# A layer of token mixing, attention and experts: the attention's end as a stage of its own, set-up in three phases, new orders on all queues

## The reference

```python
def attn(x):                                  # x: layernorm of the input
    k = x @ Wk.T; r = x @ Wr.T; v = r
    y = wkv_scan(-exp(time_decay), time_first, k, v)   # recurrence over tokens
    return (sigmoid(r) * y) @ Wo.T
def ffn(x):                                   # x: layernorm of (input + attn)
    h = rmsnorm(x, gamma1)
    q = (h @ Wq + bq); kv = (h @ Wdown + bdown) @ Wup + bup     # 16 heads of 32
    att = softmax(q k^T / sqrt(32)) over the 16 heads of one token
    x = x + (att v) @ Wo + bo
    h2 = rmsnorm(x, gamma2); gate = softmax(h2 @ Wg + bg)       # 8 experts
    return x + sum_e gate_e * (h2 @ We[e])
x = x + attn(layernorm(x)); x = x + ffn(layernorm(x))
```

## Time and profile before

| | |
|---|---|
| median of three runs | 2970.51 us |
| time of the profiled execution | 2970.13 us |
| span in that profile | 2968.3 us |
| PE matmuls busy | 2786.5 us, 94% |
| DVE busy | 2170.1 us, 73% |
| ACT busy | 1294.7 us, 44% |
| POOL busy | 610.0 us, 21% |
| mean granted TensorE clock | 0.975 |

### The profile page before, as it was taken

One profiled execution on the slowest core, in us unless ns is written; L12 is line 12 of the kernel. 1 busy time (PEld: TensorE's weight loads), 2 busy tenths in 40 slices (PEclk: granted clock), 3 DMA queues, 4 the chain that ended last, 5 costly groups with the idle time before them and its releaser, 6 DMA issues.

```text
span 2968.3 us, 47758 instructions
## 1 busy us (share of the span) xinstructions
PE 2786.5 (94%) x18896; PEld 1761.5 (59%) x18896; DVE 2170.1 (73%) x4100; ACT 1294.7 (44%) x2399; POOL 610.0 (21%) x681
## 2 busy tenths in 40 slices
PE   3269999999999999999999999999999999999989
PEld 2146566666666656666665566666556666656644
DVE  4887777877777777777777777777777777787753
ACT  1364454444444444444443444444344445344431
POOL 0122222122222212222221222122122122221210
PEclk9569999999999999999999999999999999999999
DMA  7012221112222112222211122221121221021110
GB/s 216 15 22 30 29 36 28 32 29 30 37 29 36 28 31 30 29 37 29 36 30 29 30 29 37 29 36 30 29 30 29 37 30 36 24 33 25 30 22 15
DMA packets 579074, 102.44 MB, mean 35 GB/s; under 512 B 547346, under 2 KB 547474, under 8 KB 578834
## 3 DMA queue, kind: packets, MB, share of 16 engines
q1 hardware_dynamic: 578852, 99.39, 19.4%
HBM read 48.49 MB, written 16.78 MB: 22 GB/s over the span
## 4 chain that ended last, share of the span: by engine, by line
PE 83%; DVE 6%; SPq 5%; DMA 2%; ACT 2%; issue 1%; POOL 0%; ACTq 0%; DVEq 0%
PE bank L1075 69%; PE bank L1231 8%; PE bank L1105 3%; SPq L439 3%; DVE mcol L987 3%; PE bank L1221 2%; DMA ks<-k 2%; SPq L435 2%; PE bank L1191 1%; ACT t L637 1%; PE bank L1208 1%; DVE mx L725 1%; DVE zz L915 0%; DVE w_e L823 0%; SPq L392 0%
## 5 line engine op out<-in xcount | busy, mean ns | idle before, releaser
L1075 PE MATMUL bank<-w_e,h2t 128*128 128x512 f16 x6144 | 1390.8, 382 | 5.3 <-DVE acc L1055 5.3
L1075 PEld LDWEIGHTS bank<-w_e,h2t 128*128 128x128 f16 x6144 | 598.8, 99 | 686.5 <-issue 17.5
L1055 DVE SCALAR_TENSOR_TENSOR acc<-bank,gates,acc 128x512 f32<-128x512 f32 x512 | 368.0, 729 | 246.3 <-PE bank L1075 245.7
L657 ACT ACTIVATE pr<-bank,col 128x512 f32<-128x512 f32 x256 | 171.6, 683 | 560.7 <-PE bank L1221 560.7
L1231 PE MATMUL bank<-vp,pr 128*128 128x33 f32 x2048 | 267.9, 276 | 5.1 <-ACT pr L657 5.0
L1231 PEld LDWEIGHTS bank<-vp,pr 128*128 128x128 f32 x2048 | 260.1, 196 | 17.3 <-DVE rden L1000 3.6
L476 POOL TENSOR_TENSOR zz<-wkv,zz 128x512 f32<-128x512 f32 x64 | 105.2, 1644 | 772.0 <-DVE ev L902 772.0
L1075 PE MATMUL bank<-w_o,xo 128*128 128x512 f16 x768 | 174.7, 385 | 55.6 <-DVE xo L853 55.6
L915 DVE RECIPROCAL zz<-zz 128x256 f32<-128x256 f32 x128 | 223.1, 1743 | 0.0
L987 DVE TENSOR_REDUCE mcol<-bank 128x4 f32<-128x512 f32 x256 | 155.9, 680 | 39.0 <-PE bank L1208 39.0
L1075 PE MATMUL bank<-w_o,qo 128*128 128x512 f16 x768 | 173.9, 384 | 6.4 <-DVE qo L853 6.4
(11 more groups left out here) (178 smaller groups left out, 3713.3 us busy)
## 6 DMA issues: line engine op xcount, KB each, us to landing
qs<-qo SPq DMA_DIRECT2D x384, 64.0 KB, 3.4
xk<-in_attn_x SPq DMA_DIRECT2D x32, 512.0 KB, 3.7
x<-in_attn_x SPq DMA_DIRECT2D x32, 512.0 KB, 3.7
result<-acc SPq DMA_DIRECT2D x32, 512.0 KB, 2.8
ks<-k SPq DMA_DIRECT2D x128, 64.0 KB, 3.3
w_e<-in_ffn_We SPq DMA_DIRECT2D x7, 1024.0 KB, 14.1
qs<-in_attn_Wk SPq DMA_DIRECT2D x1, 1024.0 KB, 5.8
ks<-in_attn_Wr SPq DMA_DIRECT2D x1, 1024.0 KB, 7.9
```

What stands on the lines that cost most here:

```text
L657: nc.scalar.activation(pr[:, k % 2, :], att_bank[ATT_BANK["S", k]][:, :], ACT.Exp, scale=colof["soft"])\
L1055: V.scalar_tensor_tensor(out=acc[:, s, :], in0=moe_bank[u % 2][:, :], scalar=gates[:, s, e:e + 1], in1=acc[:, s, :], op0=ALU.mult, op1=ALU ...
L1075: ins = nc.tensor.matmul(dst, left(a), right(b), start=(n == 0), stop=(n == last))
```

## The change

1. **A stage of its own.** `att_back`, `att_project`, `att_square`, `att_norm2`, `att_turn2` and `att_gate` become the stage `fin` with counters of its own. Its products O, T2 and G leave the ring of att and use the two mix banks, between V and O of the tile two later. It gets buffers of its own: `on`, `ot` (transposed output, then the second normalised tile) and `oo16`.
2. **Set-up in three phases**: k and r; then o1, q, d, u, o2, g with the constants of the attention; then the experts. Each has its own maxima, reduction over partitions, scales and counters. x and its residual copy are loaded ahead of the weights.
3. **New lists.** Each engine has a head, a repeated body and a tail. An entry (name, k, n) names a tile in the head, and a distance back from i in the body (i from 4 to 30) and from 32 in the tail.
4. The value products stay in float32, as they were.

```diff
+PHASES = [["k", "r"], ["o1", "q", "d", "u", "o2", "g"], [f"e{e}" for e in range(E)]]
+MAXED = ["k", "r", "o1", "q", "o2", "small"] + PHASES[2]
...
-            + [x for k in range(7) for x in (("S", k + 1), ("PV", k))] + [("PV", 7)]
-            + [("O", 0), ("O", 1), ("T2", 0), ("T2", 1), ("G", 0)])
+            + [x for k in range(7) for x in (("S", k + 1), ("PV", k))] + [("PV", 7)])
...
+HEAD_END, TAIL_FROM = 4, -1
...
+    ("mix_project", 0, 3), ("moe", 10, 1), ("moe", 11, 1), ("moe", 12, 1), ("att_turn", 0, 3), ("mix_turn", 0, 4),
+    ("att_latent", 0, 3),
+]
+
 PE_ORDER = [
...
+    ("att_q", 0, 1), ("mix_k", 0, 0), ("att_up", 0, 1), ("mix_v", 0, 0), ("moe", 13, 3), ("fin_project", 0, 2),
+    ("moe", 14, 3), ("att_max", 0, 1), ("att_max", 1, 1), ("moe", 15, 3), ("fin_turn2", 0, 2), ("att_max", 2, 1),
+    ("att_max", 3, 1), ("fin_gate", 0, 2), ("moe", 0, 2), ("att_m", 0, 1), ("moe", 1, 2), ("moe", 2, 2),
+    ("moe", 3, 2), ("att_scores", 0, 1), ("att_scores", 1, 1), ("moe", 4, 2), ("att_probs", 0, 1),
+    ("att_scores", 2, 1), ("att_probs", 1, 1), ("moe", 5, 2), ("att_scores", 3, 1), ("att_probs", 2, 1),
+    ("att_scores", 4, 1), ("moe", 6, 2), ("moe", 7, 2), ("att_probs", 3, 1), ("att_scores", 5, 1),
+    ("att_probs", 4, 1), ("att_scores", 6, 1), ("att_probs", 5, 1), ("att_scores", 7, 1), ("moe", 8, 2),
+    ("att_probs", 6, 1), ("att_probs", 7, 1), ("moe", 9, 2), ("mix_project", 0, 0), ("moe", 10, 2), ("moe", 11, 2),
+    ("moe", 12, 2), ("att_turn", 0, 0), ("mix_turn", 0, -1), ("att_latent", 0, 0),
 ]
...
+DVE_HEAD = [
+    ("set_init", 0, -1), ("pre_stats", 0, 0), ("pre_norm", 0, 0), ("set_max", 0, -1), ("set_max", 1, -1),
+    ("set_scale", 0, -1), ("set_max", 2, -1), ("set_k", 0, -1), ("set_max", 3, -1), ("set_max", 4, -1),
+    ("set_max", 5, -1), ("set_k", 1, -1), ("set_scale", 1, -1), ("set_r", 0, -1), ("set_r", 1, -1),
+    ("mix_turn", 0, 0), ("set_o1", 0, -1), ("set_max", 6, -1), ("set_max", 7, -1), ("set_max", 8, -1),
+    ("set_o1", 1, -1), ("mix_decay", 0, 0), ("set_q", 0, -1), ("set_max", 9, -1), ("set_max", 10, -1),
...
 DVE_ORDER = [
...
+    ("att_max", 3, 3), ("moe_gate", 0, 4), ("moe", 0, 4), ("att_m", 0, 3), ("moe", 1, 4), ("mix_rec", 0, 2),
+    ("moe", 2, 4), ("mix_rec", 1, 2), ("mix_gate", 0, 2), ("moe", 3, 4), ("mix_split", 0, 2), ("mix_decay", 1, 2),
+    ("att_probs", 0, 3), ("att_probs", 1, 3), ("moe", 4, 4), ("moe", 5, 4), ("mix_sum", 1, 2), ("mix_value", 1, 2),
+    ("mix_scan", 1, 2), ("att_probs", 2, 3), ("moe", 6, 4), ("att_probs", 3, 3), ("mix_rec", 2, 2), ("moe", 7, 4),
+    ("att_probs", 4, 3), ("mix_rec", 3, 2), ("mix_gate", 1, 2), ("att_probs", 5, 3), ("mix_split", 1, 2),
+    ("moe", 8, 4), ("att_probs", 6, 3), ("att_probs", 7, 3), ("pre_stats", 0, 1), ("moe", 9, 4),
+    ("mix_project", 0, 2), ("att_stats", 0, 2), ("moe", 10, 4), ("pre_norm", 0, 1), ("att_norm", 0, 2),
+    ("att_turn", 0, 2), ("att_latent", 0, 2), ("mix_turn", 0, 1), ("moe", 11, 4), ("fin_back", 0, 3),
+    ("mix_decay", 0, 1), ("att_stack", 0, 2), ("moe", 12, 4), ("att_vt", 0, 2), ("moe", 13, 4), ("mix_sum", 0, 1),
+    ("mix_value", 0, 1), ("fin_project", 0, 3), ("mix_scan", 0, 1), ("moe", 14, 4), ("att_max", 0, 2),
+    ("att_max", 1, 2), ("moe", 15, 4), ("fin_turn2", 0, 3), ("att_max", 2, 2),
 ]
...
 ACT_ORDER = [
...
+    ("mix_num", 1, 1), ("att_scores", 6, 2), ("att_scores", 7, 2), ("mix_split", 1, 1), ("pre_norm", 0, 0),
+    ("att_norm", 0, 1), ("att_turn", 0, 1), ("mix_turn", 0, 0), ("att_latent", 0, 1), ("att_q", 0, 1),
+    ("fin_back", 0, 2), ("mix_k", 0, 0), ("att_up", 0, 1), ("mix_v", 0, 0),
 ]
...
 POOL_ORDER = [
...
+    ("att_up", 0, 2), ("fin_square", 0, 3), ("mix_sum", 0, 1), ("moe_acc", 0, 3), ("mix_num", 0, 1),
+    ("mix_sum", 1, 1), ("mix_num", 1, 1), ("pre_stats", 0, 0), ("att_rest", 0, 2), ("att_stats", 0, 1),
+    ("att_q", 0, 1),
 ]
...
 SP_ORDER = [
-    ("mix_k", 0), ("att_up", 0), ("att_m", 0), ("pre_load", 0), ("moe_store", 0),
+    ("att_up", 0, 2), ("moe_store", 0, 4), ("att_m", 0, 2), ("mix_k", 0, 1), ("pre_load", 0, 0),
 ]
...
-        on = hrow[:, :].rearrange("p (g d) -> p g d", d=HD)
+        on = sb("on", [P, G, HD])
+        ot = sb("ot", [P, SUB * C])
...
+        oo16 = sb("oo16", [P, 2, CB, T], F16)
...
+        def pipeline(eng, head, order, tail, steps):
...
+            for name, k, n in head:
+                run(name, k, n)
+            for i in range(HEAD_END, NT + TAIL_FROM):
+                for name, k, lag in order:
+                    run(name, k, i - lag)
+            for name, k, lag in tail:
+                run(name, k, NT - lag)
...
+                if name == "small":
+                    dve.wait_ge(smalls_in, 16 * 7)
...
+                    dve.wait_ge(const_in, 16 * CONSTS)
...
-    nc = bacc.Bacc("TRN2", target_bir_lowering=False, num_devices=1)
+    nc = bacc.Bacc("TRN2", target_bir_lowering=False, num_devices=1, dynamic_dma_scratch_size=2048)
```

More of the change, by code:

```diff
@@ L128, in att_before @@
             return ATT_USES[m], True
-PE_ORDER = [
[L134 to L141, removed]
+HEAD_END, TAIL_FROM = 4, -1
@@ L142 @@
 ]
 DVE_ORDER = [
[L145 to L149, removed]
@@ L154 @@
 ]
 ACT_ORDER = [
-    ("mix_turn", 0), ("att_norm", 0), ("moe_gate", 0), ("moe", 0), ("att_turn", 0), ("moe", 1), ("mix_k", 0),
-    ("moe", 2), ("moe", 3), ("att_latent", 0), ("att_q", 0), ("att_up", 0), ("mix_v", 0), ("mix_exp", 0), ("moe", 4),
-    ("moe", 5), ("moe", 6), ("moe", 7), ("att_rest", 0), ("att_scores", 0), ("att_scores", 1), ("moe", 8),
-    ("mix_num", 0), ("mix_split", 0), ("moe", 9), ("att_scores", 2), ("att_scores", 3), ("att_scores", 4),
-    ("mix_exp", 1), ("att_scores", 5), ("moe", 10), ("att_scores", 6), ("att_scores", 7), ("moe", 11),
@@ L162 @@
[L162 to L163 removed]
+    ("mix_exp", 0, 1), ("fin_square", 0, 3), ("fin_norm2", 0, 3), ("fin_turn2", 0, 3), ("mix_num", 0, 1),
+    ("moe_gate", 0, 3), ("att_rest", 0, 2), ("att_scores", 0, 2), ("mix_split", 0, 1), ("att_scores", 1, 2),
+    ("att_scores", 2, 2), ("mix_exp", 1, 1), ("att_scores", 3, 2), ("att_scores", 4, 2), ("att_scores", 5, 2),
@@ new lines @@
+POOL_HEAD = [
+    ("set_init", 0, -1), ("pre_stats", 0, 0), ("set_bound", 0, -1), ("set_bound", 1, -1), ("mix_sum", 0, 0),
+    ("mix_num", 0, 0), ("mix_sum", 1, 0), ("mix_num", 1, 0), ("pre_stats", 0, 1), ("set_bound", 2, -1),
+    ("att_stats", 0, 0), ("att_q", 0, 0), ("att_up", 0, 0), ("mix_sum", 0, 1), ("mix_num", 0, 1), ("mix_sum", 1, 1),
+    ("mix_num", 1, 1), ("pre_stats", 0, 2), ("att_rest", 0, 0), ("att_stats", 0, 1), ("att_q", 0, 1),
+    ("att_up", 0, 1), ("fin_square", 0, 0), ("moe_acc", 0, 0), ("att_rest", 0, 1), ("mix_sum", 0, 2),
+    ("mix_num", 0, 2), ("mix_sum", 1, 2), ("mix_num", 1, 2), ("pre_stats", 0, 3), ("att_stats", 0, 2),
+    ("att_q", 0, 2),
@@ L599, in att_norm @@
                 act.wait_ge(*att_dve.done(t, "shift"))
-                if t.back(1):
-                    act.wait_ge(*att_pe.done(t.back(1), "T21"))
+                if not t.back(1):
+                    act.wait_ge(lo_done, split_done("d"))
                 for s in range(SUB):
@@ L998, in att_probs @@
                 pv = att_bank[ATT_BANK["PV", k]][:, 0:4 * (HD + 1)].rearrange("p (g d) -> p g d", g=4)
+                if k == 0 and t.back(1):
+                    dve.wait_ge(*fin_dve.done(t.back(1), "ot"))
                 dve.wait_ge(*att_pe.done(t, f"PV{k}"))
@@ L1136, in mix_turn @@
             def mix_turn(t, _):
+                if not t.back(1):
+                    pe.wait_ge(ident_in, 16)
                 pe.wait_ge(*pre_act.done(t, "norm"))
@@ L1175, in att_q @@
             def att_q(t, _):
+                if not t.back(1):
+                    pe.wait_ge(lo_done, split_done("q"))
                 for b in range(2):
@@ L1184, in att_up @@
                 pe.wait_ge(*att_dve.done(t, "c_lo"))
+                if not t.back(1):
+                    pe.wait_ge(lo_done, split_done("u"))
                 for n, use in enumerate("KV"):
```

782 lines of the change are left out of this document (469 added, 313 removed), and 3 rows, old and new, of the table ACT_HEAD.

## The result

The changed kernel takes 2944.26 us (median of 6 runs, 2943.12 to 2945.58), the kernel before 2969.86 (2963.84 to 2981.99): ratio 0.9909, 95% interval 0.9890 to 0.9928, 0.9% faster. I had said 2991, 2945 to 3025, and slower as the likeliest side. The profiled execution has a span of 2943.8 us, TensorE busy 2748.4 (93%), DVE 2172.0 (74%), mean granted clock 0.972.

A forecast was written before the change was run, and what follows sets the result against it. TensorE, busy 94% of the span, was taken as the bound. Span 2968.3 + 38 (steady waits) + 10 (clock) - 14 (start) - 12 (end) = 2990.3, plus 1.8 around it 2992, stated as 2991 us; range 2945 to 3025.

The forecast's parts named there:

- Maxima, -1.4: Products for the maxima, split into two pairs, no longer wait for reductions: 1.4 us less a tile.
- Stacking DMAs, -0.2: TensorE's wait at the maxima for the stacked keys' DMA goes: 0.2 us less a tile.
- Gate and latent, +0.9 each: Gate and latent products, each with less work between turn and product, wait 0.9 us more a tile.
- Last value product: Value product 7 waits for DVE's normalisation 5 to free its bank: 1.2 us more a tile.
- Clock, +10: New waits beside turns and value products bring six more clock falls in the steady tiles: 10 us more in total.
- the third wait: The wait forecast at value product 7 for DVE's normalisation 5: 1.2 us a tile.
- rival 3: Far slower: clock falls in nearly every tile at the turn or last value product; 3031 us, chance 0.12.
- Expert sum, 0: Store and GpSimd additions after expert product 15 end before the bank is wanted: no change taken.
- +38: Steady-state balance: added waits 3.0 minus removed waits 1.6, +1.4 us a tile, times 28.
- Start, -14: Ramp with phased set-up: first projection at 115 instead of 127.4, saving 14 us in total.
- End, -12: Last tiles: expert products cover projection and norm, saving 12 us, between 5 and 16.
- Rival 1: Faster: three new waits together 2.0 us a tile, not 3.0, total 2955; at 1.0, 2927; chance 0.22.

The follow-up runs named there:

- run 1: Changed kernel with value product 7 made to wait for DVE's normalisation 5; 3014.87 us, ratio 1.0157.
- run 5: Kernel before with expert product 12 moved between scores 7 and value product 6; 3006.40 us, ratio 1.0129.
- run 3: Changed kernel with expert product 8 moved forward, from behind scores 7 to between value product 4 and scores 6; 2957.42 us, ratio 0.9949.
- run 11: Changed kernel with start and end reordered, expert product 13 moved ahead of the latent product, and DVE's fin_turn2 ahead of its sum 15; 2960.69 us, ratio 0.9960.
- Run 8: Changed kernel with GpSimd's third reduction moved ahead of its additions and DVE's first set-up steps reordered; 2931.32 us, ratio 0.9866.
- run 4: Kernel before with its maxima in two pairs around expert product 5; 3047.85 us, ratio 1.0270.
- run 6: Changed kernel with expert product 13 moved from behind the products of v to just ahead of the latent product; 2942.00 us, ratio 0.9900.

## Why the prediction was wrong

By its steps:

**Maxima, -1.4: right.** Two pairs of 0.9 us, no wait on mcol. **Stacking DMAs, -0.2: right.** **Gate and latent, +0.9 each: right, 0.90 and 0.87 from start to start** (0.74 and 0.70 in the list); turn to product takes 2.67 again (684.85 to 687.52).

**"Last value product: a bank of value product k returns with k+2, so att_probs 7 needs normalisation 5": this step failed.** It holds up to product 6. Behind scores 7 no scores follow, so the last product takes the bank of scores 6. I counted the ring in the middle and carried it to its end. The 7.0 us of DVE behind it were right (run 1: 1.12 us), only nobody waits for them. It cost 1.2 x 28 = 34 us of the forecast, and changed its sign. (Two sums are off by one as well: 1.4 x 28 is 39, not 38, and 21 - 8 is 13, not 14.)

**Clock, +10: wrong in sign.** I counted the falls of the kernel before and asked what the new waits would add. What mattered was the cluster of short products: the change breaks it with an expert product, and the four falls behind it go (run 5 shows the same cut doing it in the kernel before, run 3 the falls coming back). The other two stood behind waits for the keys at the maxima, and went with these waits and the pairs; no run tells which of the two did it. Together some 10 us (six of 1.7). The two new waits stand at transposes and draw no fall. Had the third wait been real, rival 3's mechanism would have been too: run 1 has a fall in 21 tiles, and takes 3015. What the forecast took from the Trainium skill (TensorE: Matmul & The Clock Gate, "HAM oscillation") and set beside rival 3 isn't borne out by these 6 tiles: four of the falls stood behind no wait, and the waits of that section's example are of 3 to 5 us.

**Expert sum, 0: right, with little to spare**: in run 11 additions that start 1.6 us later already mean a wait of 0.84. DVE's gate chain does run beside GpSimd's additions in the changed kernel, one small operation taking 1.05 us instead of 0.17, there at no cost to TensorE.

So the steady state, forecast +38 and +10, came to this: in an undisturbed tile the two waits' +1.8 stand against the maxima's -1.4 and some 0.4 that the forecast has nowhere (value products 6 and 7 take 1.70 us instead of 1.92, the turn of the maxima 0.11 instead of 0.23, transposes 0.1), so 86.17 became 86.13, -1.1 in 28; and of the disturbances, 18.7 us before, the six falls (10.5) and the keys' waits (6.1) are gone and 4.4 of other kinds there: -14.3. Together -15.4.

**Start, -14: it gave 0.8.** Two waits on DVE were missing from the sum: the constants landed at 38.1, not at 33.5, and the third set of scales waited 6.62 us for a reduction that began 6.26 us after GpSimd's last addition. The profile of before shows such a gap of 5.88 us before its second reduction, a row that the forecast doesn't use. Run 8 takes both away and has its first projection at 114, where I had put it (115).

**End, -12: -8.2**, inside my -5 to -16; not counted was the gate wait of 1.8 us and its clock fall behind DVE's reciprocal.

Rival 1 (waits together 2.0 us or less, "at 1.0 it is 2927") was the nearest: they are 1.8, for which its own sum gives 2970 + 6 - 26 = 2950. That 2944 is so near is luck in part: the start and the end gave 9 and not its 26, and the disturbances, which it left as they were, gave 14.

## What to carry to other kernels

When a ring of buffers is shared by several uses, list who follows whom to the last entry; its end differs from its middle. Before a cover is moved to a new place, ask what it covers now: in a full schedule each product hides something; runs 4, 5 and 6 each moved one and lengthened another wait, and run 11 did so by moving a sum. And break clusters of short products with a wide one before taking microseconds out of waits elsewhere.
